# A perceiver layer on one core: the high part of the context is loaded by Pool's DMA queue with a cast, and ten heads' maxima go through ACT copies instead of eight

## The chip, the core and the metric

The kernel runs on one core of a Trainium2 chip. The metric is the device time of one execution in microseconds. The kernel before takes 586.85 us, the median of three runs (585.18 to 587.02 us).

## What is computed

A perceiver layer in float32 for 128 queries of width 256: cross attention to a context of 12544 rows with 16 heads of 16 dimensions, a causal self attention, and a feed-forward layer with quantised weights. Only the cross attention is touched:

```python
qh = (q @ Wq.T + bq).reshape(B, Sq, N_HEAD, D_HEAD)
kh = (k @ Wk.T + bk).reshape(B, Sk, N_HEAD, D_HEAD)      # k = v = the context, 12544 x 256
vh = (v @ Wv.T + bv).reshape(B, Sk, N_HEAD, D_HEAD)
scores = jnp.einsum('bqhd,bkhd->bhqk', qh, kh) / np.sqrt(D_HEAD)
probs = jax.nn.softmax(scores, axis=-1)
out = jnp.einsum('bhqk,bkhd->bqhd', probs, vh)
```

## The kernel before

The context is worked through in NB = 14 blocks of BK = 896 rows, and the cross attention has two stages. The first stage (to about 290 us) projects keys and values of every block, stores them to HBM scratch, and finds each head's row maximum over all keys. The second stage (290 to 520 us) reads them back, computes the scores again, their exponentials and the weighted sums. The rest, to 582 us, is self attention and the feed-forward layer. The change is in the first stage only.

To keep float32 accuracy with the faster fp32r matmuls, every operand is split into a high part (rounded to fp32r) and a low part (the rest). For block s:

- SP loads the context into `ctx_t`, a single buffer (`load`, line 245). It waits until all four pieces of block s-1 have been split (`ctx_split`).
- ACT makes the high part `ctx_hi[:, par]` by a copy (`high_context`, line 385), called by `prepare` at the start of the step before (`evacuate`, line 421). There are two such buffers, one for each parity of s.
- Pool makes the low part in four subtractions of 448 columns (`split_context`, line 326). Before piece n it waits until DVE has taken the running maximum of head `PIECE_AFTER[n]` of block s-2.
- PE works in steps of 16 slots. The table `PROJECTIONS` gives each even slot a projection: keys in slots 0, 4, 8 and 12 (two halves of each of two groups m, all through the one PSUM bank `ps_k`), values in slots 2, 6, 10 and 14. Each slot also scores one head: slots 0 to 7 score heads 8 to 15 of the last block, slots 8 to 15 score heads 0 to 7 of this one (`LAG` = 8). Three PSUM pairs rotate among the scores.
- After each key projection ACT writes `k_hi` (line 402), then DVE writes `k_lo` (`low_keys`, line 577). PE's next key projection waits for that. `k_hi` has two buffers, `k_lo` has one for each m: the first half of group m waits until SP's store of `k_lo` of the block before has landed.
- The maximum of a head is taken in one of two ways (`maximum`, line 613). Heads outside `VIA_ACT` are reduced by DVE from PSUM (line 621). Heads in `VIA_ACT` are first copied by ACT to bf16 (`copy_scores`, line 418, two staging buffers) and then joined by DVE to a running elementwise maximum (line 617), counted by `run_taken`. The running maxima are reduced once, after the last block (lines 649 and 652).

SP's queue is strictly in order. Its loop issues, for two steps at a time, the load of one block and then the stores of the block two before it:

```python
with sp.Fori(1, NB // 2) as i:
    load(i * 2, 0)
    store(i * 2 - 2, 0)
    load(i * 2 + 1, 1)
    store(i * 2 - 1, 1)
```

`store` (line 250) issues for m = 0 the store of `k_hi`, then of `k_lo`, then both for m = 1, then the values. So in step S the queue holds the load of block S+2, and behind it the stores of block S.

Of the kernel before, what the change touches and what calls it, by code (L numbers as in the profile page):

```python
# [4 lines left out]
H = 16  # L5
# [15 lines left out]
STRIDE = SLOTS + 1  # L21
SR = 96
VW = HD + 1
VIA_ACT = (1, 3, 5, 7, 9, 11, 13, 15)
NA = len(VIA_ACT)
ND = H - NA
PIECES = 4
PIECE_AFTER = (9, 11, 13, 15)
BUFFER = [[(par * H + h) % 3 for h in range(H)] for par in range(2)]

UP = 6
# [6 lines left out]
NV = len(V_TILES)  # L38
# [7 lines left out]
FT = F // P  # L46
FH = F // 2
LAG = H // 2
PREPARE_SLOTS = (5, 3)
WARM_FIRST = 14  # L50
WARM = (15, 13, 8, 10, 14, 18, 6, 2)

# [1 line left out]
def perceiver_layer(nc: bass.Bass, x_d, ctx_d, maskn_d, maskt_d, wqn_d, wqr_d, bqn_d, bqr_d, wk_d, bk_d, wv_d, bv_d,  # L54
# [9 lines left out]
    with ExitStack() as stack_of_contexts:  # L64
# [5 lines left out]
        def sem(name):  # L70
            return enter(nc.semaphore(name))
# [4 lines left out]
        ctx_t = early[:, 0:DC * BK]  # L76
# [14 lines left out]
        ctx_hi, ctx_lo = ctx_parts[:, :, 0], ctx_parts[:, :, 1]  # L91
# [61 lines left out]
        ctx_in = sem("ctx_in")  # L153
# [7 lines left out]
        out_stored = sem("out_stored")  # L161

        consts_set, row_mask_clear, wq_spread = (sem(n) for n in ("consts_set", "row_mask_clear", "wq_spread"))
        ctx_hi_ready, ctx_split, w_split = sem("ctx_hi_ready"), sem("ctx_split"), sem("w_split")
        max_copied, run_taken = sem("max_copied"), sem("run_taken")
        k_projected, v_projected, v_evacuated = (sem(n) for n in ("k_projected", "v_projected", "v_evacuated"))
        hi_ready, lo_ready = sem("hi_ready"), sem("lo_ready")
# [146 lines left out]
        @block.gpsimd  # L314
        def _(pool):
            fills = ((zeros_b[:], 0.0),
                     (early[:, o2:], 1.0),
                     (ones_c[:], 1.0), (magic[:, 0:1], MAGIC), (magic[:, 1:2], -MAGIC),
                     (k_stack[:, 0, 0:PR // 2, :].bitcast(f32), 1.0),
                     (run_late[:, :, :], LEAST),  # L320
                     (k_stack[:, 0, PR // 2:, :].bitcast(f32), 1.0))
            for n, (fill, value) in enumerate(fills[:-2]):
                nc.gpsimd.memset(fill, value).then_inc(consts_set, 1)
                pool.wait_ge(consts_set, n + 1)

            def split_context(s, par, first):

                pool.wait_ge(ctx_hi_ready, s + 1)
                for n in range(PIECES):
                    if not first:  # L330
                        pool.wait_ge(run_taken, (s - 2) * NA + VIA_ACT.index(PIECE_AFTER[n]) + 1)
                    c, half = n // 2, slice(n % 2 * HK, (n % 2 + 1) * HK)
                    nc.gpsimd.tensor_tensor(ctx_lo[:, par, c, half], ctx_t[:, c * BK:(c + 1) * BK][:, half],  # L333
                                            ctx_hi[:, par, c, half].bitcast(f32), ALU.subtract).then_inc(ctx_split, 1)

            def load_rows(s, par, first):
                if not first:
                    pool.wait_ge(mask_in[par], (s - par) * 8)
                    pool.wait_ge(max_scored, (s - 1) * H)
                pool.dma_start(mask_b[:, par, :], maskn_d[s].bitcast(u8)).then_inc(mask_in[par], 16)  # L340

            split_context(0, 0, True)
            pool.wait_ge(ctx_split, PIECES)
            load_rows(0, 0, True)
            load_rows(1, 1, True)
            for n, (fill, value) in enumerate(fills[-2:]):
                nc.gpsimd.memset(fill, value).then_inc(consts_set, 1)
                pool.wait_ge(consts_set, len(fills) - 1 + n)
            split_context(1, 1, True)
            pool.wait_ge(q_copied, 1)  # L350
            for ab in range(2):
                nc.gpsimd.tensor_scalar(q_stack[:, :, ab, :], qr, row_mask[:, ab:ab + 1], 1.0, ALU.mult,
                                        ALU.mult).then_inc(q_spread, 1)
                nc.gpsimd.tensor_scalar(qh, qr, row_mask[:, 2 + ab:3 + ab], 1.0, ALU.mult, ALU.mult).then_inc(q_spread, 1)
                pool.wait_ge(q_spread, 4 * ab + 1)
                nc.gpsimd.tensor_scalar(q_stack[:, :, ab, :], q_stack[:, :, ab, :].bitcast(f32), row_mask[:, 4:5], 1.0,
                                        ALU.mult, ALU.mult).then_inc(q_spread, 1)
                pool.wait_ge(q_spread, 4 * ab + 3)
                nc.gpsimd.tensor_tensor(q_stack[:, :, ab, :], q_stack[:, :, ab, :].bitcast(f32), qh,
                                        ALU.add).then_inc(q_spread, 1)  # L360
                pool.wait_ge(q_spread, 4 * ab + 4)
            with pool.Fori(1, NB // 2) as i:
                split_context(i * 2, 0, False)
                load_rows(i * 2, 0, False)
                split_context(i * 2 + 1, 1, False)
                load_rows(i * 2 + 1, 1, False)

            pool.wait_ge(v_projected, NB * NV)
            pool.wait_ge(ctx_split, NB * PIECES)
            nc.gpsimd.memset(k_stack[SR:SR + 1, 1, :, :].bitcast(f32), 1.0).then_inc(consts_set, 1)  # L370

            pool.wait_ge(max_scored, NB * H)
            for b in range(2):
                pool.wait_ge(mask_in[b], NB * 8)
                pool.dma_start(mask_b[:, b, :], maskt_d[b].bitcast(u8)).then_inc(mask_t_in[b], 16)
            with pool.Fori(1, NB // 2) as i:
                for par in range(2):
                    b = i * 2 + par
                    pool.wait_ge(mask_t_in[par], i * 16)
                    pool.wait_ge(scored, (b - 1) * UNITS)  # L380
                    pool.dma_start(mask_b[:, par, :], maskt_d[b].bitcast(u8)).then_inc(mask_t_in[par], 16)  # L381

        @block.scalar
        def _(act):
            def high_context(s, par):
                act.wait_ge(ctx_in, s * 16 + 16)
                nc.scalar.copy(ctx_hi[:, par].rearrange("p c k -> p (c k)"), ctx_t).then_inc(ctx_hi_ready, 1)  # L387

            high_context(0, 0)
            act.wait_ge(wqn_in, 16)  # L390
            for rows, pairs in ((wq_rows(0, 0, PR), wqn[:, 0, :]), (wq_rows(1, 0, PR // 2), wqn[:, 1, 0:D // 2]),
                                (wq_rows(1, PR // 2, PR), wqn[:, 1, D // 2:])):
# [26 lines left out]
                               ps_a[:, 2 * BUFFER[par][h]:2 * BUFFER[par][h] + 2, 0:HK]).then_inc(max_copied, 1)  # L419

            def evacuate(s, par, first, last=False):
                def prepare():

                    if not first:
                        act.wait_ge(max_scored, (s - 1) * H)
                    if not last:
                        if not (first and par == 0):
                            act.wait_ge(v_projected, s * NV)
                        high_context(s + 1, 1 - par)

                if not first:
                    prepare()
                    act.wait_ge(v_stored[par], (s - par) * 8)
                for slot, work in enumerate(PROJECTIONS):
                    if first and slot == PREPARE_SLOTS[par]:
                        prepare()
                    if work and work[0] == "v":
                        evacuate_values(s, par, work[1])
                    if work and work[0] == "k":
# [25 lines left out]
            with act.Fori(0, NB // 2) as i:  # L465
                for u in range(2 * UNITS):
                    n = i * 2 * UNITS + u
# [694 lines left out]
```

## Time and profile before

| | |
|---|---|
| median of three runs | 586.85 us |
| the profiled execution's own time | 584.14 us |
| its span (first to last instruction) | 582.5 us |
| PE busy | 532.6 us (91%) |
| ACT busy | 387.6 us (67%) |
| DVE busy | 311.1 us (53%) |
| POOL busy | 109.7 us (19%) |
| mean granted TensorE clock | 0.953 |

The rows quoted below come from one profiled execution. Busy time is that of the instructions themselves. In the lists of groups the brackets at the end give an engine's idle time before the instruction and what ended it. In the chain of waits "issue" is time for which the profile shows no wait.

### The profile page before, as it was taken

The page shows a single profiled execution, that of the slowest core. Times are in us where ns is not written, and L with a number is a line of the kernel's source. Part 1 is how long each engine was busy: PE and PEld are TensorE (multiplying, and loading weights), DVE is VectorE, ACT ScalarE, POOL GpSimd, SP SyncE. Part 2 cuts the span into 40 slices and gives each one's busy share as a digit, 9 for nine tenths or more (in the row PEclk, how much of TensorE's full clock was granted, in tenths as well). Part 3 has the DMA queues.
Part 4 walks back from the last instruction along what each step waited for, and adds up shares of the span by engine and source line. Part 5 has one row for each costly group of instructions (what it writes and reads, how often), then busy time and mean ns, then how long its engine had stood idle before and what let it go on. Part 6 is the DMA issues. An engine that isn't in the chain of part 4 may idle for free.

```text
span 582.5 us, 14289 instructions
## 1 busy us (share of the span) xinstructions
PE 532.6 (91%) x5615; PEld 436.6 (75%) x5620; DVE 311.1 (53%) x441; ACT 387.6 (67%) x404; POOL 109.7 (19%) x105
## 2 busy tenths in 40 slices
PE   5759999999999999999289999999999999979896
PEld 2648898888898888898177777777777777756543
DVE  7648898989898888899949500000000000007465
ACT  3207767777777777777268888888888888852211
POOL 9492233322233322231300000000000000000000
PEclk8569999999999999999769999999999999998799
DMA  7543655567755567693953666776766666500000
GB/s 246 176 127 130 225 189 200 213 264 272 240 181 196 212 258 272 233 410 137 368 235 101 251 237 246 272 268 258 270 221 245 226 238 242 193 3 1 1 0 9
DMA packets 34758, 117.45 MB, mean 202 GB/s; under 512 B 4400, under 2 KB 10416, under 8 KB 34736
## 3 DMA queue, kind: packets, MB, share of 16 engines
q1 hardware_dynamic: 30560, 110.58, 51.9%
q0 software_dynamic: 4032, 6.42, 4.2%
q8 instruction: 16, 0.26, 0.2%
q10 hardware_dynamic: 144, 0.13, 0.1%
q14 instruction: 6, 0.05, 0.0%
HBM read 74.44 MB, written 39.47 MB: 196 GB/s over the span
## 4 chain that ended last, share of the span: by engine, by line
PE 53%; DMA 13%; DVE 10%; issue 10%; POOL 9%; ACT 4%; POOLq 0%; SPq 0%; DVEq 0%; ACTq 0%
PE ps_a L935 21%; PE ps_k L949 18%; DMA early<-in_ctx 13%; POOL k_stack L333 9%; ACT k_stack L387 3%; PE ps_k L805 3%; PE ps_a L845 3%; PE ps_v L814 2%; PE ps_v L854 1%; PE ps_a L1041 1%; PE ps_a L879 1%; PE ps_a L1079 1%; DVE early L649 1%; DVE flag_f L604 1%; DVE peak L734 1%
## 5 line engine op out<-in xcount | busy, mean ns | idle before, releaser
L935 PE MATMUL ps_a<-q_stack,k_stack 128*128 128x256 f32 x784 | 132.1, 303 | 1.6 <-DVE q_stack L659 1.3
L935 PEld LDWEIGHTS ps_a<-q_stack,k_stack 128*128 128x128 f32 x784 | 103.3, 191 | 30.9 <-issue 29.0
L621 DVE TENSOR_REDUCE block_max<-ps_a 128x1 f32<-128x896 f32 x112 | 121.5, 1085 | 8.2 <-PE ps_a L845 5.2
L418 ACT CAST early<-ps_a 128x896 bf16<-128x896 f32 x112 | 101.5, 906 | 26.3 <-PE ps_a L845 26.0
L845 PE MATMUL ps_a<-k_hi,q_pad 128*128 128x448 f32 x448 | 110.8, 369 | 3.0 <-DVE block_max L621 3.0
L471 ACT ACTIVATE middle<-ps_a 128x1536 f32<-128x1536 f32 x70 | 94.7, 1365 | 19.4 <-PE ps_a L935 18.5
L471 ACT ACTIVATE early<-ps_a 128x1536 f32<-128x1536 f32 x70 | 94.9, 1365 | 18.7 <-PE ps_a L935 17.8
L682 DVE COPY early<-ps_k 128x512 f32<-128x512 f32 x1 | 0.7, 692 | 195.4 <-PE ps_v L988 195.4
L333 POOL TENSOR_TENSOR k_stack<-early,k_stack 128x448 fp32r<-128x448 f32 x56 | 65.5, 1173 | 156.4 <-DVE early L617 118.5
L845 PEld LDWEIGHTS ps_a<-k_hi,q_pad 128*128 128x128 f32 x448 | 79.5, 189 | 11.4 <-DVE block_max L621 4.9
L805 PE MATMUL ps_k<-k_stack,w_hi 128*128 128x448 f32 x224 | 59.9, 390 | 16.9 <-DVE k_lo L583 11.6
L814 PE MATMUL ps_v<-w_hi,k_stack 128*128 128x256 f32 x392 | 64.1, 287 | 0.0
L805 PEld LDWEIGHTS ps_k<-k_stack,w_hi 128*128 128x128 f32 x224 | 41.2, 195 | 28.0 <-DVE k_lo L583 19.3
L402 ACT ACTIVATE k_hi<-ps_k,bk 128x448 fp32r<-128x448 f32 x56 | 35.5, 633 | 38.4 <-PE ps_k L805 38.4
L814 PEld LDWEIGHTS ps_v<-w_hi,k_stack 128*128 128x128 f32 x392 | 59.0, 195 | 2.0
L617 DVE TENSOR_TENSOR early<-early 128x896 bf16<-128x896 bf16 x84 | 55.2, 658 | 4.4 <-ACT early L418 4.2
L949 PE MATMUL ps_k<-middle,v_in 128*17 128x128 f32 x1568 | 57.1, 277 | 0.0
L949 PE MATMUL ps_k<-early,v_in 128*17 128x128 f32 x1568 | 56.2, 275 | 0.0
L583 DVE SCALAR_TENSOR_TENSOR k_lo<-ps_k,bk,k_hi 128x448 fp32r<-128x448 f32 x56 | 37.7, 673 | 19.3 <-ACT k_hi L402 16.9
L949 PEld LDWEIGHTS ps_k<-middle,v_in 128*17 128x17 f32 x1568 | 37.1, 97 | 9.8 <-issue 0.2
L949 PEld LDWEIGHTS ps_k<-early,v_in 128*17 128x17 f32 x1568 | 37.0, 97 | 9.2
L381 POOL DMA_DIRECT2D mask_b<-in_maskt x12 | 6.3, 528 | 197.7 <-PE ps_a L935 197.7
(177 smaller groups left out, 460.6 us busy)
## 6 DMA issues: line engine op xcount, KB each, us to landing
k_stack<-k_hi_scratch SPq DMA_DIRECT2D x56, 448.0 KB, 6.1
v_scratch<-early SPq DMA_DIRECT2D x14, 952.0 KB, 8.0
v_in<-v_scratch SPq DMA_DIRECT2D x14, 952.0 KB, 8.9
early<-in_ctx SPq DMA_DIRECT2D x14, 896.0 KB, 6.5
k_hi_scratch<-k_hi SPq DMA_DIRECT2D x28, 448.0 KB, 6.9
k_lo_scratch<-k_lo SPq DMA_DIRECT2D x28, 448.0 KB, 6.9
k_stack<-k_lo_scratch SPq DMA_DIRECT2D x28, 448.0 KB, 6.2
mask_b<-in_maskn POOLq DMA_DIRECT2D x14, 224.0 KB, 6.6
```

Of the source, the lines that this page charges most:

```text
L333: nc.gpsimd.tensor_tensor(ctx_lo[:, par, c, half], ctx_t[:, c * BK:(c + 1) * BK][:, half], ctx_hi[:, par, c, half].bitcast(f32), ALU.subtr ...
L402: nc.scalar.activation(k_hi[:, par, m, n * HK:(n + 1) * HK], ps_k[:, 0:HK], ACT.Identity, bias=bk[:, m:m + 1]).then_inc(hi_ready, 1)
L418: nc.scalar.copy(staged[:, (par * NA + k) % 2, :].rearrange("p (n k) -> p n k", n=2), ps_a[:, 2 * BUFFER[par][h]:2 * BUFFER[par][h] + 2, 0 ...
L471: nc.scalar.activation(probs[u % SLOTS_P][:, 0:width], ps_a[:, 3 * (u % 2):3 * (u % 2) + 3, :].rearrange("p a n -> p (a n)")[:, 0:width], ...
L583: nc.vector.scalar_tensor_tensor(k_lo[:, m, half], ps_k[:, 0:HK], bk[:, m:m + 1], k_hi[:, par, m, half].bitcast(f32), ALU.add, ALU.subtrac ...
L617: nc.vector.tensor_tensor(running(h), running(h), staged[:, (par * NA + k) % 2, :], ALU.max).then_inc(run_taken, 1)
L621: nc.vector.tensor_reduce(block_max[:, par, taken:taken + 1], ps_a[:, 2 * BUFFER[par][h]:2 * BUFFER[par][h] + 2, 0:HK], AX.XY, ALU.max).th ...
L805: last = nc.tensor.matmul(ps_k[:, 0:HK], w[:, 0, c, m * P:(m + 1) * P], part[:, par, c, n * HK:(n + 1) * HK], start=(k == 0), stop=(k == l ...
L814: last = nc.tensor.matmul(ps_v[:, n * D:(n + 1) * D], part[:, par, c, t * P:(t + 1) * P], w[:, 1, c, :], start=(j == 0), stop=(j == len(te ...
L845: last = nc.tensor.matmul(out, q_pad[:, h, :], k_hi[:, par, m, n * HK:(n + 1) * HK], start=True, stop=not masked)
L935: last = nc.tensor.matmul(ps_a[:, bank, (k % 2) * 2 * Q:(k % 2 + 1) * 2 * Q], k_stack[:, b_par, a, t * P:(t + 1) * P], q_stack[:, a, :, :] ...
L949: last = nc.tensor.matmul(attended[32 * j:32 * j + VW, c * Q:(c + 1) * Q], v_ring[:, b_par, t, h, :], probs[slot][:, k * Q:(k + 1) * Q], s ...
```

## The change

The high part of the context is no longer copied by ACT. Pool issues a second load of the same block from HBM, with a cast from float32 to fp32r, straight into `ctx_hi`. It issues it in `split_context`, once the previous load into that buffer is complete and all value projections of block s-2 are done. The functions `high_context` and `prepare` go, and with them ACT's wait for the context. Heads 2, 4, 10 and 12 join `VIA_ACT`, and heads 3 and 11 leave it, so that ten heads go through ACT. `run_late` grows from two heads to four. Pool's four pieces now wait for heads 10, 13 and 15 of block s-2 and for head 2 of block s-1. SP's code is the same.

```diff
-VIA_ACT = (1, 3, 5, 7, 9, 11, 13, 15)
+VIA_ACT = (1, 2, 4, 5, 7, 9, 10, 12, 13, 15)
...
-PIECE_AFTER = (9, 11, 13, 15)
+PIECE_AFTER = ((2, 10), (2, 13), (2, 15), (1, 2))
...
-PREPARE_SLOTS = (5, 3)
...
+            pool.dma_start(ctx_hi[:, 0], ctx_d[0]).then_inc(ctx_hi_in[0], 16)
...
             def split_context(s, par, first):
 
-                pool.wait_ge(ctx_hi_ready, s + 1)
+                if not first:
+                    pool.wait_ge(ctx_hi_in[par], (s - par) * 8)
+                    pool.wait_ge(v_projected, (s - 1) * NV)
+                if not (first and par == 0):
+                    pool.dma_start(ctx_hi[:, par], ctx_d[s]).then_inc(ctx_hi_in[par], 16)
+                pool.wait_ge(ctx_in, s * 16 + 16)
+                pool.wait_ge(ctx_hi_in[par], (s - par) * 8 + 16)
                 for n in range(PIECES):
                     if not first:
-                        pool.wait_ge(run_taken, (s - 2) * NA + VIA_ACT.index(PIECE_AFTER[n]) + 1)
+                        back, head = PIECE_AFTER[n]
+                        pool.wait_ge(run_taken, (s - back) * NA + VIA_ACT.index(head) + 1)
...
-            def high_context(s, par):
-                act.wait_ge(ctx_in, s * 16 + 16)
-                nc.scalar.copy(ctx_hi[:, par].rearrange("p c k -> p (c k)"), ctx_t).then_inc(ctx_hi_ready, 1)
-
-            high_context(0, 0)
...
             def evacuate(s, par, first, last=False):
-                def prepare():
-
-                    if not first:
-                        act.wait_ge(max_scored, (s - 1) * H)
-                    if not last:
-                        if not (first and par == 0):
-                            act.wait_ge(v_projected, s * NV)
-                        high_context(s + 1, 1 - par)
-
                 if not first:
-                    prepare()
                     act.wait_ge(v_stored[par], (s - par) * 8)
```

The order on Pool's queue, in the loop over blocks, before (lines 331 to 340 are `split_context` and `load_rows`):

```order
L331 ISA [waits ctx_hi_ready]
L333 TENSOR_TENSOR k_stack<-early,k_stack 128x448 [waits run_taken]
L331 REGISTER_ALU
L333 TENSOR_TENSOR k_stack<-early,k_stack 128x448 [waits run_taken]
L331 REGISTER_ALU
L333 TENSOR_TENSOR k_stack<-early,k_stack 128x448 [waits run_taken]
L331 REGISTER_ALU
L333 TENSOR_TENSOR k_stack<-early,k_stack 128x448 [waits run_taken]
```

and the same place in the changed kernel:

```order
L331 ISA [waits ctx_hi_in0]
L333 ISA [waits v_projected]
L333 DMA k_stack<-in_ctx 128x1792
L334 ISA
L335 REGISTER_ALU [waits ctx_in]
L339 ISA [waits ctx_hi_in0]
L341 TENSOR_TENSOR k_stack<-early,k_stack 128x448 [waits run_taken]
L339 REGISTER_ALU
L341 TENSOR_TENSOR k_stack<-early,k_stack 128x448 [waits run_taken]
```

The load of `ctx_hi` (a part of `k_stack`) now stands ahead of the pieces on Pool, behind a wait for PE's value projections, and the pieces wait for both loads.

DVE's order around slots 0 and 1 of a step in the changed kernel, with the wait that both kernels have at this place (`lo_stored0` counts the landed stores of `k_lo` for m = 0):

```order
L612 TENSOR_REDUCE block_max<-ps_a 128x1 [waits max_scored]
L571 ISA
L573 REGISTER_ALU [waits hi_ready]
L574 SCALAR_TENSOR_TENSOR k_lo<-ps_k,bk,k_hi 128x448 [waits lo_stored0]
L607 ISA
L608 TENSOR_TENSOR early<-early 128x896 [waits max_copied]
```

Nothing moved in these rows. Every later maximum of the step stands behind the `k_lo` instruction.

SP's order in one step of the changed kernel, which is also that of the kernel before:

```order
L248 ISA [waits ctx_split]
L248 DMA early<-in_ctx 128x1792
L252 ISA
L253 ISA [waits hi_ready]
L253 DMA k_hi_scratch<-k_hi 128x896
L255 DMA k_lo_scratch<-k_lo 128x896 [waits lo_ready]
```

The rows are unmoved; `ctx_split`, on which the first one waits, is what Pool's four pieces count.

## Rows read from the trace of the kernel before

**Rows 1.** The page's part 4: shares of the chain of waits by line.

```profile
PE ps_a L935 21%; PE ps_k L949 18%; DMA early<-in_ctx 13%; POOL k_stack L333 9%; ACT k_stack L387 3%; PE ps_k L805 3%; PE ps_a L845 3%; PE ps_v L814 2%; PE ps_v L854 1%; PE ps_a L1041 1%; PE ps_a L879 1%; PE ps_a L1079 1%; DVE early L649 1%
```

**Rows 2.** The chain of waits, 100 to 160 us: start, us, what.

```profile
148.99 7.00 DMA early<-in_ctx
...
156.01 1.70 ACT k_stack L387
...
159.77 1.14 POOL k_stack L333
```

**Rows 3.** SP's timeline: start, us, queue, line, transfer.

```profile
166.73 0.35 SPq L248 DMA_DIRECT2D early<-in_ctx  x1
...
167.81 0.37 SPq L255 DMA_DIRECT2D k_lo_scratch<-k_lo  x1
```

**Rows 4.** Line 255, the one store issued at 167.8 us: issue to landing.

```profile
DMA to landing us min/median/max: 7.6/7.6/7.6
```

**Rows 5.** Who waited for whom, 60 to 240 us: us, times, longest.

```profile
DVE k_lo L583 <- DMA k_lo_scratch<-k_lo: 2.4, 2, 1.3
...
SPq L248 <- POOL k_stack L333: 126.2, 11, 11.9
```

**Rows 6.** DVE's timeline: start, us, line, instruction.

```profile
71.12 0.68 DVE L583 SCALAR_TENSOR_TENSOR k_lo<-ps_k,bk,k_hi 128x448 fp32r<-128x448 f32 x1 [1.33 <-DMA k_lo_scratch<-k_lo]
...
158.35 0.68 DVE L583 SCALAR_TENSOR_TENSOR k_lo<-ps_k,bk,k_hi 128x448 fp32r<-128x448 f32 x1 [1.74 <-ACT k_hi L402]
...
164.71 0.62 DVE L617 TENSOR_TENSOR run_late<-run_late,early 128x896 bf16<-128x896 bf16 x1 [0.18 <-ACT early L418]
...
175.72 0.68 DVE L583 SCALAR_TENSOR_TENSOR k_lo<-ps_k,bk,k_hi 128x448 fp32r<-128x448 f32 x1 [1.34 <-ACT k_hi L402]
...
245.91 0.68 DVE L583 SCALAR_TENSOR_TENSOR k_lo<-ps_k,bk,k_hi 128x448 fp32r<-128x448 f32 x1 [1.49 <-ACT k_hi L402]
```

**Rows 7.** PE's timeline (first three rows), then the chain of waits, 250 to 272 us.

```profile
62.21 0.57 PE L845 MATMUL ps_a<-k_hi,q_pad 128*128 128x448 f32 x2
...
159.09 1.07 PE L805 MATMUL ps_k<-k_stack,w_hi 128*128 128x448 f32 x4 [0.96 <-DVE k_lo L583]
...
166.95 0.97 PE L845 MATMUL ps_a<-k_hi,q_pad 128*128 128x448 f32 x4
...
251.20 1.22 PE ps_k L805 x6
...
267.69 1.22 PE ps_k L805 x6
```

**Rows 8.** Groups by line, 60 to 240 us: count, busy us, mean ns, idle before.

```profile
L418 ACT CAST early<-ps_a 128x896 bf16<-128x896 f32 x82 | 74.3, 907 | 16.8 <-PE ps_a L845 16.5 <-DVE early L617 0.3
...
L617 DVE TENSOR_TENSOR early<-early 128x896 bf16<-128x896 bf16 x62 | 40.2, 648 | 1.8 <-ACT early L418 1.6
```

**Rows 9.** DMA queues, 60 to 240 us: packets, MB, share of 16 engines' time.

```profile
q1 hardware_dynamic: 8692, 37.65, 57.7%
q0 software_dynamic: 1496, 2.39, 5.8%
```

**Rows 10.** Busy time by stretch: PE, PEld, DVE, ACT, POOL, granted clock, DMA.

```profile
24.00:28.00 4.00, 4.00 (x19) 3.74 (x19) 0.94 (x4) 1.68 (x2) 0.00 (x0) 0.60 0.15 59
...
32.00:38.80 6.80, 0.19 (x2) 0.09 (x2) 4.72 (x4) 0.00 (x0) 6.41 (x5) 0.65 0.62 171
...
43.00:45.00 2.00, 2.00 (x13) 2.00 (x13) 2.00 (x3) 0.85 (x1) 1.98 (x1) 0.69 0.00 0
```

**Rows 11.** PE's timeline where it resumes after idle time.

```profile
23.68 1.86 PE L805 MATMUL ps_k<-k_stack,w_hi 128*128 128x448 f32 x4 [4.15 <-DVE k_lo L583]
...
38.84 1.83 PE L805 MATMUL ps_k<-k_stack,w_hi 128*128 128x448 f32 x4 [1.99 <-issue]
```

**Rows 12.** DVE's timeline, reductions after the last block (four heads, two heads).

```profile
285.96 2.18 DVE L649 TENSOR_TENSOR early<-early 128x1792 bf16<-128x1792 bf16 x3
...
288.83 1.36 DVE L649 TENSOR_TENSOR run_late<-run_late 128x896 bf16<-128x896 bf16 x3
```

More of the change, by code:

```diff
@@ L163, in perceiver_layer @@
         consts_set, row_mask_clear, wq_spread = (sem(n) for n in ("consts_set", "row_mask_clear", "wq_spread"))
-        ctx_hi_ready, ctx_split, w_split = sem("ctx_hi_ready"), sem("ctx_split"), sem("w_split")
+        ctx_hi_in = [sem(f"ctx_hi_in{i}") for i in range(2)]
+        ctx_split, w_split = sem("ctx_split"), sem("w_split")
         max_copied, run_taken = sem("max_copied"), sem("run_taken")
@@ L421, in evacuate @@
             def evacuate(s, par, first, last=False):
-                def prepare():
-                    if not first:
-                        act.wait_ge(max_scored, (s - 1) * H)
-                    if not last:
-                        if not (first and par == 0):
-                            act.wait_ge(v_projected, s * NV)
-                        high_context(s + 1, 1 - par)
                 if not first:
-                    prepare()
                     act.wait_ge(v_stored[par], (s - par) * 8)
                 for slot, work in enumerate(PROJECTIONS):
-                    if first and slot == PREPARE_SLOTS[par]:
-                        prepare()
                     if work and work[0] == "v":
```

## The prediction, written before the changed kernel ran

> **What bounds the kernel now.** I read the chain of waits first. Over the whole span its first stage is not mainly matmuls: the load of the context alone holds 13% of the chain and Pool's pieces 9% [rows 1]. In the steady stretch the chain repeats load, ACT's high copy, the first piece, the other pieces, the next load [rows 2]. So the first stage is paced by a loop through the single buffer ctx_t. PE alone would go faster: in the last steps, where no load holds it, the same key projection (slot 8 of two successive steps) comes 16.49 us apart (251.20 to 267.69) [rows 7]. The step before that takes (245.91 - 71.12) / 10 = 17.48 us, counted on DVE's k_lo of slot 0 [rows 6]. I call that instruction t0. If only that loop went, ten intervals would give 10 x 0.99 = 9.9 us.
>
> The question is what is late next. SP's queue holds the load of block S+2 and, behind it, the stores of block S. SP sits at that load until Pool has finished its pieces: 126.2 us in 11 times [rows 5]. In the step at 158.35 Pool's last piece follows DVE's maximum of head 15 (164.71), the load goes out at 166.73, and k_lo of m = 0 only at 167.81 [rows 3, 6], although it was written before; it stood in SP's queue behind the load. It lands 7.6 us later, at 175.4 [rows 4], and DVE writes the same buffer again at 175.72 [rows 6]. The slack is 0.3 us; twice, once at 71.12, DVE did wait for this store, up to 1.3 us [rows 5, 6]. So a second loop is already as long as the first: t0, head 15, last piece, load, k_lo store, landing, next t0.
>
> **The change, part by part.**
>
> *ACT's high copy goes*: 1.70 us per step [rows 2] and ACT's wait for the load. Two more ACT copies of 0.91 us and DVE joins of 0.65 us for two reductions [rows 8] replace it. This opens the first loop. It gives nothing unless the second loop opens too, and PE's 16.49 us remain. I cost it at nothing below, covered by the second loop; if that loop were gone it would be worth the 9.9 us.
>
> *The last piece waits for head 2 of the running block (slot 10) instead of head 15 of the last one (slot 7).* This lengthens the second loop. From t0 to the taken maximum of head 2: PE restarts its slot 4 at 159.09, 0.74 us after t0, since ps_k is single, and the scores of slot 10 start at 166.95 [rows 7]. With 0.60 us for the two matmuls (the pair at 62.21 takes 0.57), 0.91 for ACT's copy and 0.65 for the join with its start [rows 7, 8], head 2 is taken at 169.1, that is t0 + 10.8. DVE's own instructions in that stretch (seven joins, three of k_lo, three reductions) are shorter in sum, so PE and ACT set it. Then, as in the trace, 0.08 to the piece's start, 1.15 for it, 0.16 to the load, 1.08 more to the k_lo store [rows 2, 3]. The sum is t0 + 13.3. In the kernel before the same sum is 167.81 - 158.35 = 9.46. So the loop is T = 13.3 + L + c, where L is the landing of that store, and c is what PE loses to a lower clock.
>
> *L.* Unchanged it is 7.6 [rows 4]. But Pool's new load of 0.917 MB is issued after slot 14's value projections. From 166.95 these are four heads' scores at 0.4, a key projection of 1.22 and a single value tile, about 0.7, further on [rows 7], so they end at 170.5, t0 + 12.2, and SP's load goes out at t0 + 12.2 too. The k_lo store then shares the DMA engines with it. On SP's queue a MB costs 57.7% x 180 / 37.65 = 2.76 us of all 16 engines; on Pool's queue, whose present loads also cast, 5.8% x 180 / 2.39 = 4.37 [rows 9]. So the new load costs 2.5 to 4.0 us, and L lies between 7.6 (it hides nothing of itself in the store's way) and 11.6. I take 7.6 + 2.5 = 10.1: both loads and the stores start together, but this cast does not change the size of an element, so SP's row is the nearer one. The Trainium skill, "DMA: Bandwidth & Descriptors", section "SWDGE vs HWDGE vs iDMA", says that software and hardware queues sit in different rings of each DMA engine, which takes them in turn. By that rule the new load gets its share before the store is through (L from 10.1), and without it, with the queues served in order of issue, L would stay 7.6. It also says that an fp32r destination always casts, which would speak for the 11.6 end.
>
> *c.* With T over 20 us and 16.5 us of work PE idles 4 us and more in one piece, at slot 4 waiting for k_lo. In the trace a gap of this kind ends at half clock: from 32.0 to 38.8 with 0.19 us of PE work the mean granted clock is 0.65 [rows 10], and the matmuls at 23.68 and 38.84 start with 1.86 and 1.83 us for four, against 1.07 at full clock [rows 7, 11]. The stretch 24 to 28 has a mean of 0.60, so the clock is low until 27.2, 3.5 us after the restart; 43 to 45 has 0.69, so low until 44.2, 5.4 us after it [rows 10, 11]. Half of that is lost: 1.75 to 2.7 us, on the path from t0 to head 2. If the clock held, 0. I take 1.75, since work restarts densely, as at 23.68.
>
> *The sum.* T = 13.3 + 10.1 + 1.75 = 25.2 us, 7.7 more than 17.48, ten times: 77. In the first full step head 2 would be scored at 62.8 (62.21 + 0.57), so taken at 64.4, the store issued 2.5 later at 66.9 and landed at 77.0, where t0 was 71.12: 5.9 more. Behind the last t0 (245.91 before) a restart at low clock once more, 1.75; the reduction of four late heads instead of two, 2.18 - 1.36 = 0.8 [rows 12] and some 0.2 in its last step; and 0.4 back in the last half step, where one more head of eight goes through ACT: 2.3. All together +85. With L = 7.6 and c = 0: T = 20.9, 3.5 + 34 + 0.6 = +38. With L = 11.6 and c = 2.7: T = 27.6, 7.5 + 101 + 3.3 = +112. The profiled execution would go from 584.14 to 669; it is 2.7 us under the median, so I put the sums on the median: 672, 625 and 699.
>
> *Edits with one answer.* At the start Pool's issue ahead of its fills moves the first pieces by about a microsecond; PE's next key projection there waits for DVE until 23.68 anyway [rows 11], with 4.15 us of idle time as cover. If the cover were gone, 1 us. The second stage and the tail are the same code.
>
> **The rivals.**
>
> - *The same loop, but the new load and the clock take little* (L up to 8.5, c up to 1): T from 20.9 to 22.8, 625 to 645 us. For it: DMA engines are idle part of each step and the clock needs some time to fall. Against it: both fall together in the burst after the load.
> - *Faster: the second loop doesn't bind.* Then PE sets the step at 16.49 and ACT's freed time is kept: 9.9 us off, 577. It decides where the k_lo store lands within 16.49 - 13.3 = 3.2 us of its issue. Against it is the 7.6 of [rows 4], and DVE's waits at that very place [rows 5]. It remains if I misread which store or which head is waited for.
> - *No change*: the gain and a store landing just as fast as needed cancel. The same number speaks against it.
> - *Pool's load paces everything.* From its issue, about t0 + 12.5 + c, until the last piece of the next step must start there are some T - 2 us, less three pieces and their waits, about 19 us. If the cast made the load take 24, T would grow by 5 more: about 720.
>
> **How the numbers follow.** A difference of 0.3% is about what a measurement of this kernel can tell from none. My forecast has 0.62, with a range of its own from 645 to 699. The loop with small additions has 0.24, the kernel paced by Pool's load 0.04, faster 0.06, no change 0.03, and slower by under 25 us 0.01. The range from 625 to 697 leaves out about two in ten. Slower by over 0.3% sums to 0.91.
>
> **What would show it.** Right: DVE's k_lo of slot 0 waits for its DMA in every step from the third, 6 us and more; the step from t0 to t0 is near 25 us; SP's load goes out 12 to 14 us after t0; landings of the k_lo store of m = 0 near 10 us; the granted clock in the steps is below 1.00, with slow matmuls after a gap. Wrong: t0 to t0 near 16.5 us and no wait on that store (the faster rival), or steps of 21 us with the clock at 1.00 (the small additions). A first stage that ends with Pool waiting for its own load would be the last rival. The second stage should still take about 230 us.

## The result, and the profile of the changed kernel

The changed kernel takes 669.0 us, the median of four runs (668.61 to 670.53), against 586.33 us for the kernel before in four runs. The ratio is 1.143, with an interval of 1.140 to 1.146. The prediction had 672 us. The profiled execution took 669.1 us; its span is 667.3 us at a mean granted clock of 0.913.

Page of the changed kernel, busy time and the chain of waits by line (parts 1 and 4):

```profile
PE 556.5 (83%) x5620; PEld 455.3 (68%) x5620; DVE 295.9 (44%) x441; ACT 386.6 (58%) x418; POOL 121.1 (18%) x119
...
PE ps_a L926 18%; DMA k_lo_scratch<-k_lo 16%; PE ps_k L940 15%; PE ps_k L796 11%; PE ps_a L836 9%; PE ps_v L805 7%; DVE k_lo L574 2%; ACT early L421 2%; PE ps_v L845 1%; DMA v_in<-in_wv 1%; PE ps_a L1032 1%; PE ps_a L870 1%; PE ps_a L1070 1%; DVE early L640 1%; DVE flag_f L595 1%
```

In [rows 1] the load of the context held 13% of the chain and Pool's pieces 9%. Both are gone from this line, and a transfer that the line did not show, the store of `k_lo`, now holds 16%.

Who waited for whom, 60 to 320 us (total us, times, longest):

```profile
POOL k_stack L341 <- DVE run_late L608: 162.1, 32, 12.1
...
DVE k_lo L574 <- DMA k_lo_scratch<-k_lo: 62.1, 10, 7.2
PE ps_k L796 <- DVE k_lo L574: 59.1, 21, 6.4
```

The wait of DVE for that store, 2.4 us in [rows 5], is 62.1 us, and PE's wait for DVE is almost the same number: PE stands still because of the store. Pool's long wait is no cost in itself; its last wait in a step is the gate that matters.

The chain of waits, 189 to 228 us, shows one whole turn and a part of the next:

```profile
189.81 0.43 PE ps_a L836 x2
...
190.39 0.91 ACT early L421
...
191.86 0.50 DVE k_lo L574
192.36 9.72 DMA k_lo_scratch<-k_lo
202.10 0.69 DVE k_lo L574
202.84 2.61 PE ps_k L796 x6
...
218.00 9.31 DMA k_lo_scratch<-k_lo
227.34 0.69 DVE k_lo L574
```

t0 is at 202.10 and 227.34. Over the run of gated steps t0 goes from 77.41 to 324.68, ten intervals of 24.73 us. SP's timeline says what the store stood behind:

```profile
216.93 0.35 SPq L248 DMA_DIRECT2D early<-in_ctx  x1
217.57 0.33 SPq L253 DMA_DIRECT2D k_hi_scratch<-k_hi  x1
218.00 0.37 SPq L255 DMA_DIRECT2D k_lo_scratch<-k_lo  x1
```

and Pool's and DVE's timelines what the load waited for:

```profile
215.62 1.15 POOL L341 TENSOR_TENSOR k_stack<-early,k_stack 128x448 fp32r<-128x448 f32 x1 [2.74 <-DVE early L608]
...
217.65 0.53 POOL L333 DMA_DIRECT2D k_stack<-in_ctx  x1 [0.38 <-issue]
```

```profile
202.10 0.68 DVE L574 SCALAR_TENSOR_TENSOR k_lo<-ps_k,bk,k_hi 128x448 fp32r<-128x448 f32 x1 [6.48 <-DMA k_lo_scratch<-k_lo]
...
207.78 0.68 DVE L574 SCALAR_TENSOR_TENSOR k_lo<-ps_k,bk,k_hi 128x448 fp32r<-128x448 f32 x1
...
214.91 0.63 DVE L608 TENSOR_TENSOR early<-early 128x896 bf16<-128x896 bf16 x1 [0.85 <-ACT early L421]
```

The `k_lo` of slot 0 is complete at 202.78 (202.10 + 0.68) and that of slot 4, the second half of the same buffer, at 208.46. The store therefore was ready to go about 9.5 us before SP issued it at 218.00. Head 2 is taken at 215.54, the last piece starts 0.08 us later and ends at 216.77, the load goes out at 216.93, the store at 218.00.

Busy time by stretch (PE, PEld, DVE, ACT, POOL, granted clock, DMA) after that restart:

```profile
202.84:206.00 3.16, 3.16 (x9) 2.81 (x10) 2.01 (x3) 0.52 (x1) 1.14 (x1) 0.50 0.77 323
206.00:208.80 2.80, 2.80 (x14) 2.71 (x13) 1.56 (x3) 1.83 (x3) 0.00 (x0) 0.53 0.00 0
208.80:211.00 2.20, 2.20 (x14) 2.06 (x13) 1.29 (x2) 1.49 (x2) 1.16 (x1) 1.00 0.00 0
```

After an idle gap of some 6 us PE resumes at half clock (1.2 of 2.4 GHz) and has the full one back by 208.8.

The 84.8 us by which the span grew lie as follows. The last gated t0 moved from 245.91 to 324.68, which is 78.8. The next slot 0 comes 19.26 us later instead of 15.91, which is 3.3. The last half step and the final reductions, which join four late maxima instead of two, take 1.3 more. The second stage and the tail have the remaining 1.4.

### The profile page after: what moved, and what is told of

Its sections match the earlier page's. It is cut to its first block, busy times and chain, and to the rows that moved or that the text cites. A ratio compares the mean times of both kernels' runs of the same rounds, so it can differ in the third digit from the quotient of the medians.

```text
span 667.3 us, 14480 instructions
## 1 busy us (share of the span) xinstructions
PE 556.5 (83%) x5620; PEld 455.3 (68%) x5620; DVE 295.9 (44%) x441; ACT 386.6 (58%) x418; POOL 121.1 (18%) x119
## 4 chain that ended last, share of the span: by engine, by line
PE 66%; DMA 17%; DVE 10%; issue 3%; ACT 3%; SPq 0%; ACTq 0%; DVEq 0%
PE ps_a L926 18%; DMA k_lo_scratch<-k_lo 16%; PE ps_k L940 15%; PE ps_k L796 11%; PE ps_a L836 9%; PE ps_v L805 7%; DVE k_lo L574 2%; ACT early L421 2%; PE ps_v L845 1%; DMA v_in<-in_wv 1%; PE ps_a L1032 1%; PE ps_a L870 1%; PE ps_a L1070 1%; DVE early L640 1%; DVE flag_f L595 1%
## 5 line engine op out<-in xcount | busy, mean ns | idle before, releaser
L421 ACT CAST early<-ps_a 128x896 bf16<-128x896 f32 x140 | 124.1, 909 | 15.8 <-PE ps_a L836 15.0
L796 PE MATMUL ps_k<-k_stack,w_hi 128*128 128x448 f32 x224 | 68.4, 435 | 76.3 <-DVE k_lo L574 69.7
L836 PE MATMUL ps_a<-k_hi,q_pad 128*128 128x448 f32 x448 | 117.3, 386 | 2.8 <-DVE block_max L612 2.7
L796 PEld LDWEIGHTS ps_k<-k_stack,w_hi 128*128 128x128 f32 x224 | 46.5, 221 | 89.6 <-DVE k_lo L574 78.4
L462 ACT ACTIVATE early<-ps_a 128x1536 f32<-128x1536 f32 x70 | 94.9, 1367 | 18.2 <-PE ps_a L926 17.3
L612 DVE TENSOR_REDUCE block_max<-ps_a 128x1 f32<-128x896 f32 x84 | 91.3, 1087 | 9.2 <-PE ps_a L836 7.3
L836 PEld LDWEIGHTS ps_a<-k_hi,q_pad 128*128 128x128 f32 x448 | 86.5, 202 | 11.4 <-DVE block_max L612 4.5
L805 PE MATMUL ps_v<-w_hi,k_stack 128*128 128x256 f32 x392 | 66.6, 295 | 0.0
L805 PEld LDWEIGHTS ps_v<-w_hi,k_stack 128*128 128x128 f32 x392 | 62.6, 206 | 2.3
L608 DVE TENSOR_TENSOR run_late<-run_late,early 128x896 bf16<-128x896 bf16 x56 | 35.3, 632 | 31.5 <-ACT early L421 31.4
L389 POOL DMA_DIRECT2D mask_b<-in_maskt x12 | 8.6, 720 | 196.0 <-PE ps_a L926 196.0
```

The lines of the kernel that those rows point to most:

```text
L421: nc.scalar.copy(staged[:, (par * NA + k) % 2, :].rearrange("p (n k) -> p n k", n=2), ps_a[:, 2 * BUFFER[par][h]:2 * BUFFER[par][h] + 2, 0 ...
L462: nc.scalar.activation(probs[u % SLOTS_P][:, 0:width], ps_a[:, 3 * (u % 2):3 * (u % 2) + 3, :].rearrange("p a n -> p (a n)")[:, 0:width], ...
L608: nc.vector.tensor_tensor(running(h), running(h), staged[:, (par * NA + k) % 2, :], ALU.max).then_inc(run_taken, 1)
L612: nc.vector.tensor_reduce(block_max[:, par, taken:taken + 1], ps_a[:, 2 * BUFFER[par][h]:2 * BUFFER[par][h] + 2, 0:HK], AX.XY, ALU.max).th ...
L796: last = nc.tensor.matmul(ps_k[:, 0:HK], w[:, 0, c, m * P:(m + 1) * P], part[:, par, c, n * HK:(n + 1) * HK], start=(k == 0), stop=(k == l ...
L805: last = nc.tensor.matmul(ps_v[:, n * D:(n + 1) * D], part[:, par, c, t * P:(t + 1) * P], w[:, 1, c, :], start=(j == 0), stop=(j == len(te ...
```

## The experiments

Each run is compared with the kernel before on the same chip (medians 584.8 to 585.65 us). T is again the spacing of t0, as the mean of the ten intervals from the third t0 to the thirteenth; it is 24.73 in the changed kernel and 17.48 before. Where a part of the change is tried by itself, the rest is the kernel named in the label.

**1. The changed kernel with the stores of m = 0 ahead of the load.** Only SP's order differs; a third argument of `store` selects the groups.

```diff
-                load(i * 2, 0)
-                store(i * 2 - 2, 0)
-                load(i * 2 + 1, 1)
-                store(i * 2 - 1, 1)
+                store(i * 2 - 2, 0, range(1))
+                load(i * 2, 0)
+                store(i * 2 - 2, 0, range(1, DC))
+                store(i * 2 - 1, 1, range(1))
+                load(i * 2 + 1, 1)
+                store(i * 2 - 1, 1, range(1, DC))
```

> The changed kernel with one edit: SP issues the stores of k_hi and k_lo of m = 0 ahead of the next context load instead of behind it. Theory (the loop through SP's queue: t0, head 2, last piece, load, k_lo store, landing, next t0): the k_lo store goes out about 5 us after t0 and has landed long before the next t0. PE then sets the step at about 16.5 us, the clock stays at full, and the time is 575 to 582 us. Rival (the new load on Pool's queue and the ten ACT copies themselves cost the time): still over 640 us.

Measured: 592.55 us, ratio 1.012 (1.009 to 1.016), T = 17.8. In the steps DVE no longer waits for a store. So 76.5 of the 82.7 us were the place of these two stores behind the load. But it missed the expected 575 to 582: something else holds T at 17.8. In the groups by line, 80 to 200 us:

```profile
L612 DVE TENSOR_TENSOR run_late<-run_late,early 128x896 bf16<-128x896 bf16 x26 | 16.2, 625 | 10.4 <-ACT early L425 10.4
...
L620 DVE TENSOR_TENSOR row_max<-row_max,block_max 128x6 f32<-128x6 f32 x7 | 7.8, 1114 | 0.0
```

DVE now waits for ACT's copies, and a tiny operation of 6 columns takes 1.11 us each. The changed kernel has it at 0.16, and so has the kernel before, with 8 columns.

**2 to 4. The three parts of the change, each without the late gate.** Run 2 is the changed kernel with its last piece gated by heads of block s-2 only; run 3 is the kernel before with the ten heads; run 4 has Pool's load with the eight heads of before, written as an edit of the changed kernel.

```diff
-PIECE_AFTER = ((2, 10), (2, 13), (2, 15), (1, 2))
+PIECE_AFTER = ((2, 10), (2, 12), (2, 13), (2, 15))
```

```diff
-VIA_ACT = (1, 3, 5, 7, 9, 11, 13, 15)
-PIECE_AFTER = (9, 11, 13, 15)
+VIA_ACT = (1, 2, 4, 5, 7, 9, 10, 12, 13, 15)
+PIECE_AFTER = (9, 12, 13, 15)
```

```diff
-VIA_ACT = (1, 2, 4, 5, 7, 9, 10, 12, 13, 15)
-PIECE_AFTER = ((2, 10), (2, 13), (2, 15), (1, 2))
+VIA_ACT = (1, 3, 5, 7, 9, 11, 13, 15)
+PIECE_AFTER = ((2, 9), (2, 11), (2, 13), (2, 15))
```

> The changed kernel with Pool's four pieces gated on heads 10, 12, 13 and 15 of the block before the last (slots 2, 4, 5 and 7) instead of ending with head 2 of the running block (slot 10). Theory: the loop is t0 + 7 (head 15) + 2.5 + landing. The load goes out at t0 + 8.4, Pool's own load at t0 + 12.4, so the k_lo store meets it only late and lands in 7.6 to 8.5 us: T = 17.1 to 18, hardly any gap on PE, full clock, 583 to 592 us. Rival (contention with Pool's load is the main cost): landing over 10 us here too, 610 us and more.

> The kernel before with the ten heads of the change through ACT copies, and nothing else (the second piece waits for head 12, as head 11 is not copied). Theory: ACT has room and head 15 still gates the last piece, so T stays at 17.3 to 17.8 and the time is 584 to 590 us. Rival (two more ACT copies per step are part of the loss): T over 18.5, over 597 us.

> The changed kernel with the eight heads of before and the pieces gated as before (heads 9, 11, 13, 15), so that only the high part's load by Pool in place of ACT's copy remains of the change. Theory: as in the run with ten heads and early pieces, T = 17.1 to 18 us, 583 to 592 us, against 17.48 before. Rival (the Pool load is the loss): over 610 us.

Measured: 603.72 us (ratio 1.032), 600.74 (1.026) and 600.71 (1.025), with intervals of at most 0.004 to each side; T is 18.8, 18.6 and 19.0. All three missed, and run 3 came out as its rival said. They agree with the main theory in that 65 of the 83 us vanish with the late gate (run 2), but neither new part is free. In the chain of waits of run 4 a new loop stands:

```profile
145.33 9.14 DMA k_stack<-in_ctx
...
155.91 1.70 POOL k_stack L341 x2
...
158.56 1.10 POOL k_stack L341
159.81 0.35 SPq L248
...
160.46 0.33 SPq L253
160.90 8.33 DMA k_lo_scratch<-k_lo
169.25 0.70 DVE k_lo L574
```

Pool issues its load only after slot 14's value projections and waits for it; then the pieces, then SP's load, then the store behind that. Run 2 has the same chain. In the kernel before, ACT's copy came early enough that the pieces went between DVE's maxima. Run 3 has no Pool load, and DVE's timeline shows one part of its cost:

```profile
133.38 1.20 DVE L617 TENSOR_TENSOR run_late<-run_late,early 128x896 bf16<-128x896 bf16 x1
```

Pool's piece runs from 132.94 to 134.09 in that trace, and this join, 0.62 us elsewhere, begins during it and takes 1.20. From 80 to 200 us the late joins take 886 ns on the mean, against 617 in the kernel before. But in the same stretch DVE also waits 12.5 us for ACT's copies, against 2.3 before; which of the two weighs more is not shown.

**5. The late gate alone.** The kernel before, with its last piece waiting for head 3 of block s-1 (head 2 is not in its `VIA_ACT`), one slot later than in the change.

```diff
-PIECE_AFTER = (9, 11, 13, 15)
+PIECE_AFTER = ((2, 9), (2, 11), (2, 13), (1, 3))
...
-                        pool.wait_ge(run_taken, (s - 2) * NA + VIA_ACT.index(PIECE_AFTER[n]) + 1)
+                        back, head = PIECE_AFTER[n]
+                        pool.wait_ge(run_taken, (s - back) * NA + VIA_ACT.index(head) + 1)
```

> The kernel before with one edit: Pool's last piece waits for head 3 of the running block (slot 11, an ACT-copied head of this kernel) instead of head 15 of the block before (slot 7). No load by Pool, eight heads as before. Theory: the late gate alone makes the large loss. Head 3 is taken 11.3 us after t0, the k_lo store goes out at t0 + 13.8 and lands 7.6 us later, and the gap on PE costs up to 1.75 us of clock: T = 21.5 to 23.5 us, 628 to 648 us. Rival (the Pool load must be there for the large loss): under 605 us.

Measured: 652.88 us, ratio 1.115 (1.112 to 1.118), T = 23.96. The gate alone costs 67 us; that is a little over the expected range, and the way is not the expected one. In this kernel the chain runs through the load and ACT's copy, and the wait for the store ends last in one of six steps only (80 to 230 us):

```profile
DVE k_lo L584 <- ACT k_hi L403: 29.7, 5, 7.3
...
DVE k_lo L584 <- DMA k_lo_scratch<-k_lo: 6.2, 1, 6.2
```

**6. The changed kernel without Pool's steady loads.** `ctx_hi` is loaded for the first two blocks only, so the later high parts are those of old blocks.

```diff
+                if first and par == 1:
+                    pool.dma_start(ctx_hi[:, par], ctx_d[s]).then_inc(ctx_hi_in[par], 16)
                 if not first:
-                    pool.wait_ge(ctx_hi_in[par], (s - par) * 8)
                     pool.wait_ge(v_projected, (s - 1) * NV)
-                if not (first and par == 0):
-                    pool.dma_start(ctx_hi[:, par], ctx_d[s]).then_inc(ctx_hi_in[par], 16)
                 pool.wait_ge(ctx_in, s * 16 + 16)
-                pool.wait_ge(ctx_hi_in[par], (s - par) * 8 + 16)
+                if first:
+                    pool.wait_ge(ctx_hi_in[par], 16)
```

> The changed kernel without Pool's loads of the high part from block 2 on (the blocks then use the high parts of blocks 0 and 1; this part of the computation is left out). All waits for heads and for SP's load stay. Theory: the k_lo store of m = 0 lands in 7.6 us again instead of 9.2 to 9.7, the clock cost stays, T falls from 24.9 to about 23.0, and the time from 669 to 647 to 653 us. Rival (the burst takes no share from the store; the 9.5 us are because the m = 1 stores now stand close behind it): landing over 9 us still, over 663 us.

Measured: 653.92 us, ratio 1.114 (1.110 to 1.119), T = 23.5; both are slightly above the expected 647 to 653 us and 23.0. The store of `k_lo` of m = 0 lands in 7.4 to 8.1 us where the changed kernel has 9.1 to 10.4 (on the mean 7.7 and 9.4). Pool's load costs 15 us, some 1.2 us a step: the landing is 1.7 shorter, but the store goes out 0.5 later after t0 (15.7 instead of 15.2), and why it does is open.

**7. The changed kernel with its clock kept up.** Before slot 4 PE does 22 matmuls on zeros, into `ps_v`, while it would wait for `k_lo`.

```diff
                     for slot in which:
+                        if slot == 4:
+                            pe.wait_ge(v_evacuated, s * NV + 1)
+                            keep_clock(ps_v[:, :], 22)
                         project(s, par, slot)
```

> The changed kernel with 22 matmuls on zeros into ps_v (4.7 us at full clock) ahead of the key projection of slot 4 of each step, where PE idles 5 to 6.5 us; they wait only for the value copy of slot 2. Theory: the clock stays at full through the gap, the path from t0 to head 2 shrinks by the 1.7 to 2.6 us that the low clock cost, T = 22.3 to 23.3 us in the gated steps. Two steps have no such gap and get up to 4.7 us longer, so the time is 648 to 660 us. Rival (the low clock is off the path): T stays at 24.9 and the time goes up to 672 to 680 us.

Measured: 658.22 us, ratio 1.124 (1.121 to 1.127), T = 22.90. PE's timeline:

```profile
169.69 4.92 PE L845 MATMUL ps_v<-zeros_b 128*128 128x512 bf16 x22
175.10 1.08 PE L796 MATMUL ps_k<-k_stack,w_hi 128*128 128x448 f32 x4 [0.49 <-DVE k_lo L574]
```

Four matmuls take 1.08 us after the wait, where the changed kernel has 1.86, and the landings stay at 9.2 to 9.7 us. The lower clock therefore costs 24.73 - 22.90 = 1.83 us a step. PE does more work and the kernel is 11 us faster.

**8. The kernel before with the stores of m = 0 ahead of the load.** The diff is that of run 1, on the kernel before.

> The kernel before with SP's stores of m = 0 issued ahead of the context load. The loop through SP's queue goes, the loop through ctx_t (head 15, pieces, load, ACT's copy, k_hi, k_lo) stays at about 17.4 us if the load still takes 6.6 us, and less if it lands earlier with no stores right behind it. Theory: T = 16.5 to 17.3, 577 to 585 us. Rival (the loop through SP's queue did not bind before): no change, 585 to 587 us.

Measured: 572.75 us (572.31 to 574.33), ratio 0.978 (0.976 to 0.981), T = 16.57. This is faster than both kernels and better than the expected 577 to 585. The chain of waits in the steady part holds PE alone, which is busy 180.0 of the 180 us from 60 to 240. SP's timeline, then who waited for whom (60 to 240 us), then DMA issues of 60 to 210 us (KB, median us to landing):

```profile
156.82 0.33 SPq L253 DMA_DIRECT2D k_hi_scratch<-k_hi  x1
158.43 0.33 SPq L255 DMA_DIRECT2D k_lo_scratch<-k_lo  x1
162.12 0.35 SPq L248 DMA_DIRECT2D early<-in_ctx  x1
```

```profile
DVE k_lo L587 <- ACT k_hi L406: 5.4, 11, 0.8
...
ACT k_stack L391 <- DMA early<-in_ctx: 0.4, 2, 0.2
```

```profile
early<-in_ctx SPq DMA_DIRECT2D x9, 896.0 KB, 5.6
k_hi_scratch<-k_hi SPq DMA_DIRECT2D x18, 448.0 KB, 2.7
k_lo_scratch<-k_lo SPq DMA_DIRECT2D x18, 448.0 KB, 2.6
```

The store goes out 3.7 us before the load and lands in 2.5 us, not 7.6 [rows 4]. I had expected the loop through `ctx_t` to stay and hold T at 16.5 to 17.3. It does not bind either, because the load too lands sooner once the stores of m = 0 are out of its burst: 5.6 us against 6.6 as the median of the kernel before. ACT's wait for it is 0.4 us in total.

**9. Pool's load with eight heads, stores first.** Run 4 with run 1's diff.

> Eight heads, early pieces, the high part loaded by Pool (the run with the Pool load alone), and SP's stores of m = 0 ahead of the context load. Theory: the long chain there was slot 14's values, Pool's load (9.2 us), four pieces (6.4), SP's load, k_lo store (8.3), t0. Without the store in it, pieces end some 16.3 us after slot 14, just ahead of PE's next-but-one step (about 17.2): T = 16.5 to 16.8, 571 to 578 us, no better than ACT's copy with the same order of stores (572.75). Rival (Pool's load costs by itself): over 583 us.

Measured: 585.81 us (12 runs), ratio 0.999 (0.997 to 1.001), T = 17.6. A miss, on the rival's side: 13 us slower than run 8, which differs from it in Pool's load and in what goes with it. From the trace, engines in order of start:

```profile
182.78 4.86 POOL L345 TENSOR_TENSOR k_stack<-early,k_stack 128x448 fp32r<-128x448 f32 x4 [8.78 <-DMA k_stack<-in_ctx]
...
183.44 0.97 DVE L612 TENSOR_TENSOR run_late<-run_late,early 128x896 bf16<-128x896 bf16 x1 [0.33 <-ACT early L425]
...
184.34 1.12 DVE L620 TENSOR_TENSOR row_max<-row_max,block_max 128x8 f32<-128x8 f32 x1
```

By the time the load has landed, all four gates are open, so the pieces run back to back for 4.86 us, and DVE's joins fall into them.

**10. The late gate with the stores first.** Run 5 with run 1's diff.

> The kernel before with the late last piece (head 3 of the running block) and SP's stores of m = 0 ahead of the load. Theory: the late gate lengthens both loops, and this leaves only that through ctx_t: 12.7 us to the load, 6 for it, 2.4 for ACT's copy and k_hi, up to 1.9 of clock: T = 21 to 23.3, 620 to 645 us. Rival (SP's queue is the only way in which the late gate hurts): under 590 us.

Measured: 654.15 us, ratio 1.117 (1.113 to 1.120), T = 24.05. It is slower than expected and no faster than run 5. The chain of waits says why:

```profile
162.43 1.16 POOL k_stack L338
...
163.75 6.25 DMA early<-in_ctx
170.00 0.02 issue
170.02 1.69 ACT k_stack L392
```

With ACT's copy still there, the late gate lengthens the first loop just as much: last piece, load, ACT's copy. ACT executes in order, so its `k_hi` of the step stands behind that copy: DVE waits 29.7 us in five times for `k_hi`, up to 7.6 us each (80 to 200 us). Run 1 has a gate only one slot earlier, but no ACT copy, and T is 17.8. So the change did open the first loop, and widely; the second one swallowed it.

**11. Ten heads, stores first.** Run 3 with run 1's diff.

> The kernel before with ten heads through ACT and SP's stores of m = 0 ahead of the load. Theory: the ten-head order has a limit of its own (two neighbouring heads through ACT's copies, the maxima behind them and the rotation of three PSUM pairs), seen as 17.7 us per step in the changed kernel with stores first: T = 17.6 to 18.5, 585 to 600 us. Rival (that residue came from Pool's load): T = 16.6, 572 to 577 us.

Measured: 593.42 us, ratio 1.013 (1.009 to 1.016), T = 17.8, as expected and the same as run 1. With the stores first in both, ten heads cost 593.42 - 572.75 = 20.7 us. DVE's waits for ACT's copies, 3.7 us in run 8 over 60 to 240 us, are

```profile
DVE run_late L621 <- ACT early L422: 12.7, 19, 1.0
DVE early L621 <- ACT early L422: 11.5, 20, 0.9
```

and the late joins take 831 ns on the mean where run 8 has 616 (80 to 200 us). I did not separate these two.

**12. Run 9 with the pieces spread.** The last three pieces wait for heads 1 and 3 of the running block, so that they can't run together.

```diff
-PIECE_AFTER = ((2, 9), (2, 11), (2, 13), (2, 15))
+PIECE_AFTER = ((2, 15), (1, 1), (1, 3), (1, 3))
```

> As the run with the Pool load, eight heads and stores first (585.8 us, 17.4 us per step), but with the pieces gated on head 15 of the block before the last and heads 1, 3 and 3 of the running block. There the four pieces ran back to back as soon as Pool's load had landed, on top of DVE's joins of two SBUF operands: the row_max instruction took 1.00 us on average instead of 0.16, with DVE busy 95% of the time. Theory (that collision is the Pool load's remaining cost): row_max is back at 0.16 us, T = 16.5 to 16.9, 573 to 579 us. Rival (the 0.9 MB more of transfers, or pieces that are late for PE, cost the step): T stays at 17.2 or more, 583 us and more.

Measured: 582.79 us (12 runs), ratio 0.996 (0.994 to 0.997), T = 17.15. Groups by line of 80 to 200 us, then PE's timeline and PE's wait for Pool from 60 to 240 us:

```profile
L620 DVE TENSOR_TENSOR row_max<-row_max,block_max 128x8 f32<-128x8 f32 x7 | 1.1, 159 | 0.0
```

```profile
188.35 1.08 PE L800 MATMUL ps_k<-k_stack,w_hi 128*128 128x448 f32 x4 [0.49 <-POOL k_stack L345]
```

```profile
PE ps_k L800 <- POOL k_stack L345: 5.7, 11, 0.7
```

`row_max` is back at 159 ns from 983 in run 9, so the collision with Pool was what stretched it. It has moved in part: the joins into `early` take 707 ns here, 680 in run 9 and 647 in run 8. The gain is 2 to 3 us of the 13 (3.0 between the medians, 2.2 by the ratios), short of the expected 573 to 579: the pieces now end too late and PE waits about 0.5 us for the last one in every step. That is nearly all by which T is above run 8's (17.15 against 16.57, 5.8 us over ten steps). Of the other 4 us the last step holds 2.7 (the last t0 comes 18.59 us after the one before it, in run 8 15.92); why it does was not tried. No version with Pool's load came near run 8.

## Why the prediction was right

**The loop.** The prediction named the chain: t0, head 2, last piece, SP's load, the `k_lo` store behind it, its landing, the next t0. It stands in the trace link by link, and run 1 removes it by moving the two stores of m = 0 in one queue, with 76.5 us. Run 2 shows the late gate as its cause: without it 65 us are gone. Run 5 does not show it for this loop: there the same gate costs 67 us, but through the load and ACT's copy, and with the stores first it costs as much (run 10).

**Its terms.** The issue of the store was taken as t0 + 13.3 plus c = 1.75, so 15.05; it is 15.0 at 177.34 (192.36) and 15.9 at 202.10 (218.00), and 15.2 on the mean of the ten. c is 1.83 by run 7, inside the range of 0 to 2.7. L was taken as 10.1 and is 9.1 to 10.4, 9.4 on the mean: the choice of the nearer row, SP's queue, was right in kind, and L 0.7 too long. The rival of small additions (L up to 8.5 and c up to 1) is refuted in both of its terms, and Pool's load, landing in 9.5 us at the median, is far from the 24 of the last one. In 60 to 320 us Pool's queue takes 13.1% x 260 / 11.73 = 2.9 us of all 16 engines per MB, close to the 2.76 of SP's queue and far from the 4.37 of Pool's mask loads [rows 9], although the mask loads are still among them:

```profile
q1 hardware_dynamic: 8865, 38.49, 39.7%
q0 software_dynamic: 3028, 11.73, 13.1%
```

Of the 2.5 us that the load was to add to L, run 6 finds 1.7 in the landing and 1.2 in the step. Together T was put at 25.2 and is 24.73, so ten intervals gave 72.5 instead of 77. (The sum's upper end was 699 us, the stated range ends at 697; nothing hangs on it.) The queues do share: by the Trainium skill, "DMA: Bandwidth & Descriptors", section "SWDGE vs HWDGE vs iDMA", each DMA engine takes its rings in turn. Run 6 agrees in direction, with landings of 7.4 to 8.1 us where the changed kernel has 9.1 to 10.4.

**The ends.** The first gated t0 was to come at 77.0 and came at 77.41. Behind the last one I had 2.3 us, and the trace has 6.0. The clock after the last restart was undersized: the step after it costs 3.3 us more than before where I took 1.75. In run 7, with the clock kept up, the same step takes 16.80 us instead of 19.26, so 2.5 of the 3.3 are the clock; the other 0.9 (16.80 against 15.91) are left for what I had put at nothing. The two errors nearly cancel: 4.5 too much in the intervals, 3.7 too little at the end, 0.4 too little at the start. The sum was +85, the spans differ by 84.8. That the total came within 3 us is partly luck; that the loop came within half a microsecond a step is not.

**The step that failed.** "I cost it at nothing below, covered by the second loop; if that loop were gone it would be worth the 9.9 us." The first half holds nearly, as far as the time goes; the second is wrong, and with it the time that the faster rival gave. With the loop gone (run 1) the changed kernel is at 592.55, not at 577. Ten heads through ACT cost 15 us by themselves (run 3) and 21 with the loops open (run 11); I had counted two copies and two joins as busy time on engines with room, and neither the order in which DVE waits for ACT's copies between reductions nor the joins that a piece on Pool stretches; how the cost divides between these two is open. Pool's load costs 15 us by itself (run 4): it opens a chain of its own through the pieces and the same queue. Behind the loop that I found, smaller limits were waiting, all above the 16.49 us of PE: the ten heads' order, the chain of Pool's load, and Pool's pieces beside DVE's joins.

**The kernel before.** The prediction had 0.3 us of slack between its two loops and called the first the pace. Run 8 shows that one edit of the second loop's order relaxes both, since their transfers share a burst. A row that shows a load of 7.0 us does not say what it would take with other neighbours.

## What to carry to other kernels

In an in-order DMA queue, put every transfer that is already ready ahead of one that waits for a late gate. Here a changed order of a few calls brought 13 us to the kernel before and 76 to the changed one. When a change moves a gate to a later slot, follow every transfer queued behind what it gates, up to the buffer that it frees, and add the turn up as t0 to t0. Work taken off an engine earns nothing until that sum is below the busiest engine's, and each new loop has to be looked for after the first one is open: try the parts alone and on top of the fix.

## What the runs showed of the hardware beyond what was expected

- **A DVE instruction with two SBUF inputs takes longer beside a Pool subtraction.** A 128x8 `TENSOR_TENSOR` went from 0.16 to 1.12 us, a 128x896 join from 0.62 to 1.20, while a piece of 1.15 us ran on Pool; the reductions from PSUM stayed at 1.09. The Trainium skill, "SBUF — State Buffer", section "Who interferes with whom", says that such a pair of instructions contends for a shared port and that the one that comes second blocks; runs 3, 9 and 12 agree with their numbers above.
- **The landing of a store depends on what is issued beside it.** The same 448 KB of `k_lo` landed in 2.5 us when sent ahead of the load (run 8), 7.4 to 8.1 behind it, and 9.1 to 10.4 with Pool's load in the burst as well. With Pool's load, but ahead of SP's (run 1), it was 4.6 to 5.5.
- **Filling a gap with matmuls on zeros paid.** In run 7 the granted clock of the steps is 1.00, and 4.92 us of useless work per step took 11 us off the kernel. It repairs a symptom only: run 1 has no such gap and is 66 us faster still.
